# Attention heads on one core: value products in pairs of key steps instead of one step at a time

## The chip, the core and the metric

The kernel runs on one core of a Trainium2 chip. The metric is the time of one execution on the device in microseconds (us). Inputs and outputs are in DRAM, the arithmetic must be that of the reference in float32 accuracy, and everything is one program of six phases.

## What is computed

Six blocks one after another on `x` of 4 x 1024 tokens with 256 features, each adding to `x`: half a mixture of 16 experts, attention with biases, half the mixture again, half a lookup-table network, attention without biases, and half the lookup-table network again. The change touches the two attention blocks:

```python
q = (jnp.einsum('btc,oc->bto', x, Wq) + bq).reshape(Bb, Tt, H, D).transpose(0, 2, 1, 3)
...
logits = jnp.einsum('bhqd,bhkd->bhqk', q, k) / jnp.sqrt(jnp.float32(D))
causal = jnp.triu(jnp.ones((Tt, Tt), dtype=bool), 1)
logits = jnp.where(causal, -jnp.inf, logits)
attn = jax.nn.softmax(logits, axis=-1)
out = jnp.einsum('bhqk,bhkd->bhqd', attn, v)
```

There are 16 heads of 16 features, 4 batches and 1024 positions.

## The kernel before

`attention_phase` has a projection phase and then `heads_phase`, which is run twice in the program (tiles `attn_heads_...`). It works by quads: four heads of one batch, 16 quads (`NQ`) one after another. A quad holds two kinds of score products, both in bfloat16 parts stacked to a depth of 96 or 99.

- **Row scores** (`unit`, line 1101): 32 units per quad, one for each head and block of 128 queries, in the order `QUERY_ORDER = (5, 4, 1, 2, 7, 6, 0, 3)` for each head. Unit of block i has (i + 1) x 128 columns, 128 to 1024, so one product or two (at most 512 columns each), and fills one or two of the four banks of `s_ps`. VectorE (line 1299) reduces each to its row maxima. The units run a whole quad ahead: while quad n has its turned scores, the units of quad n+1 (and the first 9, `LEAD`, of n+2) are issued. In a line of the 32 units that are issued during a quad, number d (from 0) is unit 9 + d, counted around: d = 4 has 896 columns, then 128, 512, 768, 640, 256, 384, 1024 and again 896, 128, and so on. `unit` waits on `s_free` until VectorE has left the banks; `score_banks` gives each unit its banks in a ring, so that a unit of two banks waits for the last unit that had them.
- The maxima of a quad are split on GpSimd (`split_max`), turned by one product (`turn_max`, line 1111, once per quad), copied by VectorE and stored by a DMA into the stacked operands.
- **Turned scores** (`scores_t`, line 1120): 12 key steps (`STEPS`), 4 for the first half of the queries and 8 for the second, times 4 heads are 48 pieces. Widths of the steps: 512, 384, 256, 128, then five times 512, then 384, 256, 128. They go through three banks of `st_ps` (`NB`): piece p waits until ScalarE has taken the exponential of piece p - 3 (line 1218). The results go to `probs`, a ring of four steps (`NR`): the exponentials of step G wait until the value products of step G - 4 are done. On the diagonal steps (0 to 3 and 8 to 11) GpSimd then masks (line 1043).
- **Value products** (`times_v`, line 1136): per step one group, four products (one for each head), which the chip executes as eight float32 passes. The four heads stand in the four 32-column strips of TensorE and stream side by side. A group waits for the step's exponentials or mask. Each half of a quad gathers in the one bank `o_ps`, which ScalarE copies out (`copy_out`, line 1200), at the pieces in `COPY_AFTER`.

The order on TensorE is written out by three tables. After piece p (0 to 47) come the units until `PACE[p]` of them are issued, and then the value groups that `VALUES_AFTER` names for p, relative to the quad's step 0:

```python
PACE = (0, 0, 1, 2, 4, 4, 4, 5, 5, 7, 7, 7, 8, 9, 10, 11, 11, 11, 12, 13, 14, 15, 15, 16, 16, 17, 17, 18, 20, 20, 21,
        21, 23, 24, 24, 25, 25, 26, 27, 28, 28, 28, 28, 28, 29, 29, 31, 32)
```

In the last quad of a phase no units are left, and the output projection (`project`, line 1157) stands in their place. The operands of a quad (`stack0`, `more_st`) are loaded by SP two quads ahead, from the time when the turned scores of quad n begin, and the units of quad n+2 need them from piece 32 of quad n on.

Of the kernel before, what the change touches and what calls it, by code (L numbers as in the profile page):

```python
# [687 lines left out]
def step_queries(half, j):  # L688

    first = max(half * TILE, j * P)  # L690
    return first, (half + 1) * TILE - first
# [3 lines left out]

PACE = (0, 0, 1, 2, 4, 4, 4, 5, 5, 7, 7, 7, 8, 9, 10, 11, 11, 11, 12, 13, 14, 15, 15, 16, 16, 17, 17, 18, 20, 20, 21,
        21, 23, 24, 24, 25, 25, 26, 27, 28, 28, 28, 28, 28, 29, 29, 31, 32)
COPY_AFTER = (9, 28)
VALUES_AFTER = {2: -3, 5: -2, 8: -1, 12: 0, 18: 1, 22: 2, 25: 3, 31: 4, 35: 5, 38: 6, 41: 7, 44: 8}


def score_banks(quads, banks):
# [54 lines left out]
def heads_phase(nc, name, before, q_dram, k_dram, v_sb, stack0, first_loaded, o_dram, inv_dram, x_in, x_out, w_o, b_o, consts):  # L757
# [5 lines left out]
    NQ = BATCH * QUADS  # L763
    UNITS = QUAD * QT
    PIECES = QUAD * len(STEPS)
    S = len(STEPS)
# [26 lines left out]
    def masks_until(G):  # L793
        n, s = divmod(G, S)
        return n * len(DIAGONAL) + sum(d <= s for d in DIAGONAL)

    with ExitStack() as ctx:
# [130 lines left out]
        with nc.Block() as block:  # L928
# [161 lines left out]
            def _(pe):  # L1090
                def unit(g):
                    n, k = divmod(g, UNITS)
                    h, i = k // QT, QUERY_ORDER[k % QT]
                    r, (at, _, over) = n % R, UNIT_AT[g]
                    if k == 0:
                        pe.wait_ge(stack_loaded[r], LOAD * (n // R + 1))
                    if over:
                        pe.wait_ge(s_free, over)
                    for a in range(0, (i + 1) * P, TILE):
                        w = min(TILE, (i + 1) * P - a)  # L1100
                        last = pe.matmul(s_ps[:, at + a // TILE, 0:w], q_st(r)[0:DEPTH, h, i * P:(i + 1) * P],  # L1101
                                         k_st(r)[0:DEPTH, h, a:a + w], start=True, stop=True)
                    last.then_inc(s_full, 1)
                    if k == TURN_AFTER and n > 0:
                        turn_max(n - 1)

                def turn_max(m):
                    at, _, over = TURN_AT[m]
                    pe.wait_ge(parts_ready, m + 1)
                    pe.wait_ge(s_free, over)  # L1110
                    pe.matmul(s_ps[0:SPLIT * UNITS, at, 0:P], max_parts[:, m % 2, :], identb[:, :],
                              start=True, stop=True).then_inc(s_full, 1)

                def scores_t(n, s, h):
                    half, j = STEPS[s]
                    first, w = step_queries(half, j)
                    v = n * PIECES + s * QUAD + h
                    if v >= NB:
                        pe.wait_ge(exp_done, v - NB + 1)
                    pe.matmul(st_ps[:, v % NB, 0:w], k_st(n % R)[0:ROWS, h, j * P:(j + 1) * P],  # L1120
                              q_st(n % R)[0:ROWS, h, first:first + w], start=True, stop=True).then_inc(st_full, 1)

                def times_v(G):
                    n, s = divmod(G, S)
                    half, j = STEPS[s]
                    first, w = step_queries(half, j)
                    use = 2 * n + half
                    if j == 0 and use >= OB:
                        pe.wait_ge(o_free, use - OB + 1)
                    if s in DIAGONAL:  # L1130
                        pe.wait_ge(masked, masks_until(G))
                    else:
                        pe.wait_ge(exp_done, QUAD * (G + 1))
                    for h in range(QUAD):
                        at = ((n * QUAD + h) * QT + j) * VW
                        last = pe.matmul(o_ps[h * VW:(h + 1) * VW, use % OB, TILE - w:TILE], v_sb[:, at:at + VW],  # L1136
                                         probs[:, G % NR, h, 0:w], start=(j == 0), stop=(s in (SUB - 1, S - 1)))
                    last.then_inc(pv_done, 1)

                def project(q):  # L1140

                    t, s = divmod(q, SUB)
                    u = q // 2
                    if q == 0:
                        pe.wait_ge(w_ready, 1)
                        pe.wait_ge(s_free, turn_over(NQ - 1))
                    pe.wait_ge(lo_ready, KD * t + (1 if t == TILES - 1 else KD))
                    if u >= SB and q % 2 == 0:
                        pe.wait_ge(y_free, u - SB + 1)
                    toks = slice(s * P, (s + 1) * P)  # L1150
                    for kd in range(KD):
                        if t == TILES - 1 and kd == 1:
                            pe.wait_ge(lo_ready, KD * TILES)
                        pairs = [(rows_hi[:, t % 2, kd, toks], w_hi[:, kd, :]), (rows_hi[:, t % 2, kd, toks], w_lo[:, kd, :]),
                                 (rows_lo[:, t % 2, kd, toks], w_hi[:, kd, :])]
                        for n, (a, b) in enumerate(pairs):
                            last = pe.matmul(s_ps[:, u % SB, s % 2 * D:(s % 2 + 1) * D], a, b, start=(kd == 0 and n == 0),
                                             stop=(kd == KD - 1 and n == len(pairs) - 1))
                    if q % 2 == 1:
                        last.then_inc(y_full, 1)  # L1160
# [4 lines left out]
                for n in range(NQ):  # L1165
                    pe.wait_ge(neg_loaded[n % 2], 16 * (n // 2 + 1))
                    due = 0
                    for s in range(S):
                        for h in range(QUAD):
                            scores_t(n, s, h)  # L1170
                            p = s * QUAD + h
                            while due < PACE[p]:
                                g = (n + 1) * UNITS + LEAD + due
                                if g < NQ * UNITS:
                                    unit(g)
                                elif g == NQ * UNITS + TURN_AFTER:
                                    turn_max(NQ - 1)
                                due += 1
                            if p in VALUES_AFTER and n * S + VALUES_AFTER[p] >= 0:
                                times_v(n * S + VALUES_AFTER[p])  # L1180
                            if n == NQ - 1 and p in PROJECT_AFTER:
                                project(PROJECT_AFTER[p])
                for G in range((NQ - 1) * S + max(VALUES_AFTER.values()) + 1, NQ * S):
                    times_v(G)
                for q in range(len(PROJECT_AFTER), SUB * TILES):
                    project(q)
# [7 lines left out]
            def _(act):  # L1194
                def copy_out(n, half):
                    act.wait_ge(pv_done, n * S + (SUB if half == 0 else S))
                    if n > 0:

                        act.wait_ge(o_stored[half], 16 * n)
                    act.activation(oT[:, half, :], o_ps[:, (2 * n + half) % OB, :], ACT.Copy).then_inc(o_free, 1)  # L1200
# [8 lines left out]
                for n in range(NQ):  # L1209
                    for s, (half, j) in enumerate(STEPS):  # L1210
# [4 lines left out]
                        for h in range(QUAD):  # L1215
# [3 lines left out]
                                .then_inc(exp_done, 1)  # L1219
                            if s * QUAD + h == COPY_AFTER[0] and n > 0:  # L1220
                                copy_out(n - 1, 1)
                            if s * QUAD + h == COPY_AFTER[1]:
                                copy_out(n, 0)
# [1485 lines left out]
```

## Time and profile before

| | us |
|---|---|
| median of 3 runs | 2773.62 (2769.53 to 2778.78) |
| span of the profiled execution | 2889.1 |
| TensorE busy | 2486.6 (86%) |
| VectorE busy | 1963.1 (68%) |
| ScalarE busy | 1445.2 (50%) |
| GpSimd busy | 1097.0 (38%) |

The profiled execution's own time is the span of 2889.1 us, from its first to its last instruction; what lies around it is not shown. It is 115 us longer than the median of the runs without the profiler. The two heads phases lie at about 780 to 1240 us and 2165 to 2640 us of the span. Matmuls are pipelined, so their durations overlap; the distance between two starts tells what one costs.

### The profile page before, as it was taken

The numbers are of one execution on the slowest core, as the hardware profiler recorded it, in microseconds if no ns is written. First come the engines' busy times: TensorE is split into PE (matmuls) and PEld (weight loads), VectorE is DVE, ScalarE is ACT, GpSimd is POOL, SyncE is SP. The second block draws the span as 40 slices with busy tenths as digits, with TensorE's granted clock in tenths as the row PEclk, the third lists the DMA queues.
The fourth block names the chain that finished last, engine by engine and source line by source line (L and its number), as shares of the span: only waits on it lengthen the run. The fifth ranks groups of instructions, "written<-read, shape, count | busy, mean of one in ns | idle before, by whom it ended". The sixth has DMA issues, their size and how long they took to land. (4 is left out here: it accounts for less than half of the span.)

```text
span 2889.1 us, 49366 instructions
## 1 busy us (share of the span) xinstructions
PE 2486.6 (86%) x15174; PEld 1604.9 (56%) x15190; DVE 1963.1 (68%) x5524; ACT 1445.2 (50%) x3366; POOL 1097.0 (38%) x1556
## 2 busy tenths in 40 slices
PE   7885997788799999968868994899679999996998
PEld 5664996455333333446648993677553333334776
DVE  6654887665688888656646884665568887875444
ACT  3332554232287877723324552333546887874443
POOL 5663444776322222335653446662132222220000
PEclk9997998898799999978989996999788999998999
DMA  3435555555534464343345554331473354434000
GB/s 119 150 123 145 179 179 174 157 165 171 130 85 92 95 128 93 85 159 124 126 131 170 178 178 148 98 107 48 143 178 68 78 116 99 99 96 154 30 32 27
DMA packets 251508, 350.78 MB, mean 121 GB/s; under 512 B 42437, under 2 KB 200694, under 8 KB 245110
## 3 DMA queue, kind: packets, MB, share of 16 engines
q1 hardware_dynamic: 212854, 242.71, 32.2%
q0 software_dynamic: 38400, 104.91, 10.3%
q8 instruction: 132, 2.16, 0.3%
q14 instruction: 122, 1.00, 0.1%
HBM read 196.80 MB, written 149.92 MB: 120 GB/s over the span
## 5 line engine op out<-in xcount | busy, mean ns | idle before, releaser
L1299 DVE CUSTOM_DVE_ANT_0 attn_heads_masked_s<-attn_heads_s_ps,attn_heads_causal 128x768 bf16<-128x768 f32 (+7 forms) x1024 | 726.7, 754 | 143.6 <-PE attn_heads_s_ps L1101 126.6
L1218 ACT ACTIVATE attn_heads_probs<-attn_heads_st_ps 128x512 f32<-128x512 f32 (+3 forms) x1536 | 663.4, 495 | 234.1 <-PE attn_heads_st_ps L1120 220.2
L1609 POOL DMA_INDIRECT xs_dram<-moe_route_xn,rows_at x256 | 262.0, 1023 | 182.3 <-DVE rows_at L1877 110.4
L1136 PE MATMUL attn_heads_o_ps<-attn_heads_probs,attn_v_sb 128*32 128x512 f32 (+3 forms) x3072 | 329.1, 501 | 2.1 <-POOL attn_heads_probs L1043 1.9
L1043 POOL TENSOR_SCALAR_AFFINE_SELECT attn_heads_probs<-attn_heads_probs 128x512 f32<-128x512 f32 x256 | 163.0, 637 | 364.5 <-ACT attn_heads_probs L1218 359.3
L1120 PE MATMUL attn_heads_st_ps<-attn_heads_more_st 99*128 99x512 bf16 x960 | 261.7, 330 | 0.1
L1101 PE MATMUL attn_heads_s_ps<-attn_heads_more_st 96*128 96x512 bf16 (+1 forms) x960 | 246.7, 335 | 9.8 <-DMA attn_heads_more_st<-k_dram 4.8
L2105 POOL DMA_DIRECT2D ys_dram<-moe_expert_y_sb x288 | 157.3, 546 | 244.7 <-DVE moe_expert_y_sb L2223 244.2
L1120 PEld LDWEIGHTS attn_heads_st_ps<-attn_heads_more_st 99*128 99x128 bf16 x960 | 84.5, 97 | 212.7 <-ACT attn_heads_probs L1218 159.7
L2137 PE MATMUL moe_expert_gu_ps<-moe_w_hi,moe_expert_xT_hi 128*128 x576 | 189.4, 329 | 0.9 <-DVE moe_expert_xT_lo L2205 0.7
L1101 PE MATMUL attn_heads_s_ps<-attn_stack 96*128 96x512 bf16 (+2 forms) x576 | 157.6, 358 | 27.6 <-DVE attn_heads_row_max L1299 11.3
L2179 ACT ACTIVATE moe_expert_xT_hi<-moe_expert_xT_ps 128x256 fp32r<-128x256 f32 x288 | 110.7, 384 | 132.7 <-PE moe_expert_xT_ps L2123 132.2
L97 POOL DMA_INDIRECT attn_stack<-ys_dram,rows_at x128 | 147.5, 1152 | 62.9 <-issue 36.1
L2137 PE MATMUL moe_expert_gu_ps<-moe_w_hi,moe_expert_xT_lo 128*128 x576 | 164.1, 285 | 0.0
L2137 PE MATMUL moe_expert_gu_ps<-moe_w_lo,moe_expert_xT_hi 128*128 x576 | 164.0, 285 | 0.0
L97 POOL DMA_INDIRECT lut_y_sb<-ys_dram,rows_at x128 | 132.7, 1036 | 76.3 <-issue 36.1
L1120 PE MATMUL attn_heads_st_ps<-attn_stack 99*128 99x512 bf16 (+3 forms) x576 | 159.7, 335 | 0.9 <-ACT attn_heads_probs L1218 0.7
L2564 DVE SCALAR_TENSOR_TENSOR lut_hid<-lut_gate,lut_u_ps 128x512 f32<-128x512 f32 x80 | 54.9, 687 | 151.8 <-PE lut_u_ps L2397 111.8
L2205 DVE TENSOR_TENSOR moe_expert_xT_lo<-moe_expert_xT_ps,moe_expert_xT_hi 128x256 fp32r<-128x256 f32 x288 | 122.2, 424 | 50.4 <-ACT moe_expert_xT_hi L2179 47.0
L2486 ACT ACTIVATE lut_gate<-lut_g_ps 128x512 f32<-128x512 f32 x96 | 57.2, 595 | 188.2 <-PE lut_g_ps L2397 167.0
L411 PE MATMUL attn_proj_w_ps<-attn_proj_mask,attn_proj_diag 128*128 128x512 bf16 x416 | 110.2, 420 | 47.2 <-DVE attn_proj_mask L595 43.3
L2123 PE MATMUL moe_expert_xT_ps<-ident,moe_expert_x_sb 128*128 128x128 f32 x576 | 113.4, 279 | 38.2 <-DMA moe_expert_x_sb<-xs_dram 34.8
(276 smaller groups left out, 6137.0 us busy)
## 6 DMA issues: line engine op xcount, KB each, us to landing
moe_expert_x_sb<-xs_dram SPq DMA_DIRECT2D x288, 128.0 KB, 2.1
ys_dram<-moe_expert_y_sb POOLq DMA_DIRECT2D x288, 128.0 KB, 2.1
o_dram<-attn_heads_oT SPq DMA_DIRECT2D x64, 256.0 KB, 5.7
moe_route_w_raw<-in_L_ffn_we_dram SPq DMA_DIRECT2D x96, 128.0 KB
q_dram<-attn_proj_parts SPq DMA_DIRECT2D x32, 384.0 KB, 2.8
k_dram<-attn_proj_parts SPq DMA_DIRECT2D x32, 384.0 KB, 2.7
x_mid<-moe_route_x_sb SPq DMA_DIRECT2D x16, 512.0 KB
attn_v_sb<-o_dram SPq DMA_DIRECT2D x32, 256.0 KB
```

The lines of the kernel that those rows point to most:

```text
L97: pool.indirect_dma_start(y_sb[:, r, k, :], None, ys_dram, bass.IndirectOffsetOnAxis(rows_at[:, u, k:k + 1], 0))\
L1043: pool.affine_select(out=d, in_=d, compare_op=ALU.is_ge, fill=0.0, base=0, pattern=[[0, QUAD], [1, P]], channel_multiplier=-1).then_inc(ma ...
L1101: last = pe.matmul(s_ps[:, at + a // TILE, 0:w], q_st(r)[0:DEPTH, h, i * P:(i + 1) * P], k_st(r)[0:DEPTH, h, a:a + w], start=True, stop=True)
L1120: pe.matmul(st_ps[:, v % NB, 0:w], k_st(n % R)[0:ROWS, h, j * P:(j + 1) * P], q_st(n % R)[0:ROWS, h, first:first + w], start=True, stop=Tr ...
L1136: last = pe.matmul(o_ps[h * VW:(h + 1) * VW, use % OB, TILE - w:TILE], v_sb[:, at:at + VW], probs[:, G % NR, h, 0:w], start=(j == 0), stop ...
L1218: act.activation(probs[:, G % NR, h, 0:w], st_ps[:, v % NB, 0:w], ACT.Exp, scale=scale)\
L1299: dve.tensor_tensor_reduce(out=masked_s[:, use % 4, 0:w], in0=s_banks[:, at * TILE:at * TILE + w], in1=causal[:, SEQ - w:SEQ], scale=1.0, ...
L1609: pool.indirect_dma_start(xs_dram, bass.IndirectOffsetOnAxis(rows_at[:, n * SUB + s, k:k + 1], 0), xn[:, n % RX, s, :], None).then_inc(sca ...
L2105: pool.dma_start(ys_dram[s * P:(s + 1) * P, :], y_sb[:, s % AHEAD, :]).then_inc(y_stored[s % AHEAD], 16)
L2123: last = pe.transpose(xT_ps[:, s % 2, kd * P:(kd + 1) * P], x_sb[:, s % AHEAD, kd * P:(kd + 1) * P], ident[:, :])
L2137: last = pe.matmul(gu_ps[:, s % 2, 0:D], a, b, start=(n == 0), stop=(n == len(pairs) - 1))
L2205: dve.tensor_tensor(xT_lo[:, s % RH, :, :].rearrange("p k t -> p (k t)"), xT_ps[:, s % 2, 0:D], xT_hi[:, s % RH, :, :].rearrange("p k t -> ...
```

## The change

Two tables and the loops that read them. Value groups stand after six pieces of a quad, two at each, instead of one after each of twelve pieces; the copy of the first half moves from piece 28 to piece 25. The instructions on ScalarE, VectorE, GpSimd and SP are the same in the same order, except for that copy's place. `PACE` and the number of instructions stay as they are.

```diff
-COPY_AFTER = (9, 28)
-VALUES_AFTER = {2: -3, 5: -2, 8: -1, 12: 0, 18: 1, 22: 2, 25: 3, 31: 4, 35: 5, 38: 6, 41: 7, 44: 8}
+COPY_AFTER = (9, 25)
+VALUES_AFTER = {6: (-2, -1), 14: (0, 1), 22: (2, 3), 30: (4, 5), 38: (6, 7), 46: (8, 9)}
...
-                            if p in VALUES_AFTER and n * S + VALUES_AFTER[p] >= 0:
-                                times_v(n * S + VALUES_AFTER[p])
+                            for step in VALUES_AFTER.get(p, ()):
+                                if n * S + step >= 0:
+                                    times_v(n * S + step)
...
-                for G in range((NQ - 1) * S + max(VALUES_AFTER.values()) + 1, NQ * S):
+                for G in range((NQ - 1) * S + max(VALUES_AFTER[max(VALUES_AFTER)]) + 1, NQ * S):
                     times_v(G)
```

TensorE, pieces 10 to 14 of a quad (`s_ps` row scores, `st_ps` turned scores, `o_ps` value products; the widths behind the names; x4 is one group of four heads). Before:

```order
L1101 MATMUL attn_heads_s_ps<-attn_heads_more_st 128x512
L1120 MATMUL attn_heads_st_ps<-attn_stack 128x256 x2
L1120 MATMUL attn_heads_st_ps<-attn_stack 128x128
L1101 MATMUL attn_heads_s_ps<-attn_heads_more_st 128x512
L1101 MATMUL attn_heads_s_ps<-attn_heads_more_st 128x256
L1136 MATMUL attn_heads_o_ps<-attn_heads_probs,attn_v_sb 32x512 x4
L1120 MATMUL attn_heads_st_ps<-attn_stack 128x128
L1101 MATMUL attn_heads_s_ps<-attn_heads_more_st 128x512
L1101 MATMUL attn_heads_s_ps<-attn_heads_more_st 128x128
L1120 MATMUL attn_heads_st_ps<-attn_stack 128x128
L1101 MATMUL attn_heads_s_ps<-attn_heads_more_st 128x256
```

And with the change:

```order
L1101 MATMUL attn_heads_s_ps<-attn_heads_more_st 128x512
L1120 MATMUL attn_heads_st_ps<-attn_stack 128x256 x2
L1120 MATMUL attn_heads_st_ps<-attn_stack 128x128
L1101 MATMUL attn_heads_s_ps<-attn_heads_more_st 128x512
L1101 MATMUL attn_heads_s_ps<-attn_heads_more_st 128x256
L1120 MATMUL attn_heads_st_ps<-attn_stack 128x128
L1101 MATMUL attn_heads_s_ps<-attn_heads_more_st 128x512
L1101 MATMUL attn_heads_s_ps<-attn_heads_more_st 128x128
L1120 MATMUL attn_heads_st_ps<-attn_stack 128x128
L1101 MATMUL attn_heads_s_ps<-attn_heads_more_st 128x256
L1136 MATMUL attn_heads_o_ps<-attn_heads_probs,attn_v_sb 32x512 x4
L1136 MATMUL attn_heads_o_ps<-attn_heads_probs,attn_v_sb 32x384 x4
```

The group of step 0 moved from behind piece 12 to behind piece 14, and that of step 1 joined it there; the row scores of 640 and 256 columns now stand ahead of both.

TensorE again, pieces 38 to 41, with the groups of steps 6 and 7. Before:

```order
L1120 MATMUL attn_heads_st_ps<-attn_heads_more_st 128x384
L1101 MATMUL attn_heads_s_ps<-attn_heads_more_st 128x384
L1136 MATMUL attn_heads_o_ps<-attn_heads_probs,attn_v_sb 32x512 x4
L1120 MATMUL attn_heads_st_ps<-attn_heads_more_st 128x384
L1101 MATMUL attn_heads_s_ps<-attn_heads_more_st 128x512 x2
L1120 MATMUL attn_heads_st_ps<-attn_heads_more_st 128x256 x2
L1136 MATMUL attn_heads_o_ps<-attn_heads_probs,attn_v_sb 32x512 x4
L1120 MATMUL attn_heads_st_ps<-attn_heads_more_st 128x256 x2
```

And with the change:

```order
L1120 MATMUL attn_heads_st_ps<-attn_heads_more_st 128x384
L1101 MATMUL attn_heads_s_ps<-attn_heads_more_st 128x384
L1136 MATMUL attn_heads_o_ps<-attn_heads_probs,attn_v_sb 32x512 x8
L1120 MATMUL attn_heads_st_ps<-attn_heads_more_st 128x384
L1101 MATMUL attn_heads_s_ps<-attn_heads_more_st 128x512 x2
L1120 MATMUL attn_heads_st_ps<-attn_heads_more_st 128x256 x4
L1120 MATMUL attn_heads_st_ps<-attn_heads_more_st 128x128
```

The group of step 7 moved from behind piece 41 to behind piece 38, and between that run and the next one stand pieces 39 to 46 alone with their units.

## Rows read from the trace of the kernel before

**Rows 1.** The page, part 1: busy us (share of the span) and instructions.

```profile
PE 2486.6 (86%) x15174; PEld 1604.9 (56%) x15190; DVE 1963.1 (68%) x5524; ACT 1445.2 (50%) x3366; POOL 1097.0 (38%) x1556
```

**Rows 2.** Timeline of TensorE, maxima products: start us, us, engine, line, operation.

```profile
1002.23 0.22 PE L1111 MATMUL attn_heads_s_ps<-identb,attn_heads_max_parts 128*96 128x128 bf16 x1
...
1028.92 0.22 PE L1111 MATMUL attn_heads_s_ps<-identb,attn_heads_max_parts 128*96 128x128 bf16 x1
```

**Rows 3.** One quad: length; PE, PEld, DVE, ACT, POOL busy; PEclk, DMA share, GB/s.

```profile
1002.23:1028.92 26.69, 26.69 (x195) 9.53 (x194) 22.95 (x65) 21.43 (x51) 5.98 (x12) 1.00 0.41 81
```

**Rows 4.** Waits in that quad: waiter, releaser, us in total, times, longest.

```profile
ACT attn_heads_probs L1218 <- PE attn_heads_st_ps L1120: 5.5, 11, 1.0
DVE attn_heads_masked_s L1299 <- PE attn_heads_s_ps L1101: 3.7, 10, 1.0
...
PEld attn_heads_s_ps L1101 <- DVE attn_heads_row_max L1299: 0.9, 4, 0.3
```

**Rows 5.** Timeline of TensorE, pieces 12 to 22 of a quad.

```profile
1014.42 1.06 PE L1136 MATMUL attn_heads_o_ps<-attn_heads_probs,attn_v_sb 128*32 128x512 f32 x8
1015.42 0.23 PE L1120 MATMUL attn_heads_st_ps<-attn_heads_more_st 99*128 99x128 bf16 x1
...
1017.39 0.85 PE L1136 MATMUL attn_heads_o_ps<-attn_heads_probs,attn_v_sb 128*32 128x384 f32 x8
...
1019.27 0.38 PE L1101 MATMUL attn_heads_s_ps<-attn_stack 96*128 96x512 bf16 x1
1019.49 0.38 PE L1120 MATMUL attn_heads_st_ps<-attn_heads_more_st 99*128 99x512 bf16 x1
1019.80 0.64 PE L1136 MATMUL attn_heads_o_ps<-attn_heads_probs,attn_v_sb 128*32 128x256 f32 x8
1020.37 0.39 PE L1120 MATMUL attn_heads_st_ps<-attn_heads_more_st 99*128 99x512 bf16 x1
```

**Rows 6.** Timeline of TensorE and its weight loads, end of the first phase.

```profile
1232.44 1.79 PE L1136 MATMUL attn_heads_o_ps<-attn_heads_probs,attn_v_sb 128*32 128x384 f32 x24
1232.79 0.13 PEld L1136 LDWEIGHTS attn_heads_o_ps<-attn_heads_probs,attn_v_sb 128*32 128x32 f32 x4 [0.19 <-issue]
1233.11 0.13 PEld L1136 LDWEIGHTS attn_heads_o_ps<-attn_heads_probs,attn_v_sb 128*32 128x32 f32 x4 [0.19 <-issue]
```

**Rows 7.** Timeline of VectorE; in brackets its idle time before.

```profile
1012.81 1.09 DVE L1299 CUSTOM_DVE_ANT_0 attn_heads_masked_s<-attn_heads_s_ps,attn_heads_causal 128x896 bf16<-128x896 f32 x1 [0.25 <-PE attn_heads_s_ps L1101]
...
1013.83 0.29 DVE L1299 CUSTOM_DVE_ANT_0 attn_heads_masked_s<-attn_heads_s_ps,attn_heads_causal 128x128 bf16<-128x128 f32 x1
...
1014.04 0.69 DVE L1299 CUSTOM_DVE_ANT_0 attn_heads_masked_s<-attn_heads_s_ps,attn_heads_causal 128x512 bf16<-128x512 f32 x1
...
1015.96 0.82 DVE L1299 CUSTOM_DVE_ANT_0 attn_heads_masked_s<-attn_heads_s_ps,attn_heads_causal 128x640 bf16<-128x640 f32 x1 [0.35 <-PE attn_heads_s_ps L1101]
...
1016.71 0.42 DVE L1299 CUSTOM_DVE_ANT_0 attn_heads_masked_s<-attn_heads_s_ps,attn_heads_causal 128x256 bf16<-128x256 f32 x1
...
1017.05 0.55 DVE L1299 CUSTOM_DVE_ANT_0 attn_heads_masked_s<-attn_heads_s_ps,attn_heads_causal 128x384 bf16<-128x384 f32 x1
...
1017.53 1.22 DVE L1299 CUSTOM_DVE_ANT_0 attn_heads_masked_s<-attn_heads_s_ps,attn_heads_causal 128x1024 bf16<-128x1024 f32 x1
```

**Rows 8.** Timeline of ScalarE, exponentials, merged by threes.

```profile
1008.64 1.57 ACT L1218 ACTIVATE attn_heads_probs<-attn_heads_st_ps 128x512 f32<-128x512 f32 x3 [0.33 <-PE attn_heads_st_ps L1120]
...
1014.25 0.84 ACT L1218 ACTIVATE attn_heads_probs<-attn_heads_st_ps 128x256 f32<-128x256 f32 x3
```

**Rows 9.** Timelines of TensorE and VectorE where a bank is waited for.

```profile
935.77 0.28 PE L1101 MATMUL attn_heads_s_ps<-attn_stack 96*128 96x256 bf16 x1
...
935.64 0.82 DVE L1299 CUSTOM_DVE_ANT_0 attn_heads_masked_s<-attn_heads_s_ps,attn_heads_causal 128x640 bf16<-128x640 f32 x1
```

**Rows 10.** Second phase: TensorE behind a stack's arrival, and its clock after.

```profile
2442.87 0.82 PE L1101 MATMUL attn_heads_s_ps<-attn_heads_more_st 96*128 96x512 bf16 x2 [3.80 <-DMA attn_heads_more_st<-k_dram]
...
2443.00:2446.00 3.00, 3.00 (x14) 0.81 (x12) 1.80 (x4) 1.08 (x2) 0.64 (x1) 0.50 0.02 7
```

## The prediction

> **What bounds the kernel now.** I read the page first: TensorE is busy 86% of the span, VectorE 68%, ScalarE 50% [rows 1]. That is an average over six phases, so I went on to the only stretches that the edit touches, the two heads phases of 16 quads each (about 800 to 1235 and 2180 to 2626 us). The turned maxima, one product per quad, mark the period: 26.69 us from one to the next [rows 2]. In such a quad TensorE has no gap (26.69 us busy of 26.69) and the granted clock is 1.00, VectorE is busy 22.95 and ScalarE 21.43 [rows 3]. The waits of the same quad say how near the other two are: VectorE stands idle 3.7 us for want of scores, ScalarE 5.5 us, and TensorE's score products wait 0.9 us for banks [rows 4]. So TensorE bounds the quad, with VectorE 14% behind and ScalarE 20%, and these two are fed out of rings that hold little: four banks of row scores for VectorE (two units, roughly), three of turned scores for ScalarE.
>
> **What is removed.** In the timeline of TensorE [rows 5] 512-wide score products start 0.22 us apart, but the value product behind one starts 0.31 us after it: 0.09 us to change over. Four heads' value products of 512 columns take 1.00 us to the next product's start, those of 256 columns 0.57: 0.43 per 256 columns and 0.14 beside. One changeover and back is 0.09 + 0.14 = 0.23 us, and the rows are rounded, so 0.24. Do two groups one behind the other save it? The end of the phase shows it [rows 6]: there three groups already stand together. The second group's weight loads, one pass ahead of its products, start at 1232.79 and 1233.11, 0.32 us apart, which is one 384-column pass and nothing more ((0.43 x 1.5) / 2). So the whole 0.24 us goes. Per phase there are 190 changeovers (16 x 12, less two joined at the end), and 96 after. 2 x 94 x 0.24 = 45 us of TensorE's own time, 1.44 us per quad, to 25.25. The Trainium skill, TensorEngine Tiling (Array Packing), Key Properties, says that changing the tiling mode drains the engine; by that rule alone the change gives these 45 us, and the trace agrees that the drain is there. That is my first rival, not my forecast.
>
> **What is added: gaps in the supply.** No instruction is added, and no DMA is moved. But the two feeds now stop for both groups together: steps 0,1 for 0.09 + 0.85 + 0.64 + 0.14 = 1.73 us; 2,3 for 0.88; 4,5 and 6,7 for 1.95; 8,9 for 1.73; 10,11 for 0.88. Before, the longest stop was 1.00 + 0.09 = 1.09 us. VectorE needs, unit following unit, 1.02 us for 896 columns, 0.75 for 640, 0.48 for 384, 0.34 for 256, 0.21 for 128 [rows 7], and by the same slope 0.61 for 512, 0.88 for 768 and 1.15 for 1024. ScalarE needs 0.49 us per 512 columns (three in 1.57, the last one alone 0.60) and about 0.28 per 256 [rows 8]; by interpolation 0.39 for 384 and 0.17 for 128, and 0.5 for a copy. TensorE streams 0.22 us per 512 columns [rows 5], others in proportion.
>
> I walked one quad of the new order by these numbers, always in order: a product starts when its engine is free and its bank is (0.12 us after VectorE, 0.15 after ScalarE), the reader starts 0.2 us after the product's stream. The latencies are read so: piece 13 starts at 1015.42, its 0.06 us and the 0.27 of the 640-column unit behind it end at 1015.75, and VectorE begins that unit at 1015.96 [rows 5, 7], 0.2 later; VectorE left the 768-column unit at 935.64 and the product that needed its bank began at 935.77, 0.13 later [rows 9]. ScalarE's 0.15 is my estimate by the latter. The worst stretch, pieces 7 to 14, counted from the end of the run of steps 10,11: VectorE still works until 0.22; TensorE streams piece 7 and the 896-column unit until 0.55, so VectorE idles to 0.75 and has it until 1.77; the 128 and 512 units follow until 2.58. The 768 unit needs the banks of the 896 one, so it starts at 1.89 though TensorE was ready at 1.65; VectorE has it from 2.58 to 3.46. The 640 unit waits for the 512 one (2.70), the 256 one for the 768 one: it starts at 3.58, TensorE having been ready at 3.03. Only then, at 3.78, can the run of steps 0,1 start, and it ends at 5.42. TensorE's own work there is 0.79 (turned scores) + 1.36 (six units) + 1.73 = 3.88 us. 1.5 us are lost, and while the run lasts VectorE has 0.75 + 0.34 us left to do and then nothing: it idles near 1.3 us.
>
> The other stretches by the same walk, TensorE's own time and the walk's: pieces 15 to 22, 3.71 and 4.37; 23 to 30, 5.37 and 6.14 (here ScalarE, with the copy after piece 25 in its way, holds back pieces 29 and 30); 31 to 38, 4.73 and 5.32 (ScalarE, idle at the start since its three banks last 1.5 us of a 1.95 us run); 39 to 46, 3.60 and 4.26; 47 to 6, 3.60 and 4.02. Sum: 24.9 own, **29.53 us per quad**, against 26.69: +2.84. The loss comes from how little is buffered, not from the engines' rates. As a test I walked pieces 13 to 22 of the old order likewise: it gives 2.40 us between the runs of steps 1 and 2, and in the trace they lie 2.41 apart (1017.39 and 1019.80 of rows 5).
>
> **The sum.** Units are issued alongside in 14.6 quads of each phase: 2 x 14.6 x 2.84 = +83 us. The last quad of a phase has no units and saves up to 6 x 0.24 = 1.4 us, twice: -3. The stack of a later quad arrives late in some quads: in the second phase TensorE stood 3.80 us for it, and behind that the clock granted to it was 0.50, half of the 2.4 GHz [rows 10]; two such quads there, two smaller ones in the first phase. A slower quad reaches the stack's first unit some 2.5 us later, so the waits shrink: about -1 in the first phase, -5 in the second, and perhaps -3 for products no longer streamed at the lower clock. Together +71 us. Against the profiled execution's span of 2889.1 us that is 2960; the unprofiled median is 2773.6, 115 us less, and since the heads phases run at full clock there I take their change over unscaled: **2844 us**, +2.6%. Other costs I put at nothing: the ring of four probability tiles (a step's slot is freed by a run ahead of the piece that needs it, at each of the six places), GpSimd's masks (0.64 us each, done over 1 us before the run that reads them), the move of the copy from piece 28 to 25 (inside the walk). If the masks lost that cover, it would be tenths of a us per quad.
>
> Bounds: nothing here shows a run of two long groups beside VectorE's feed, so the lower end is that half of the walk's waits are overstated (+1.4 per quad: +41, less 7, so +34, 2808), and the upper that each latency is 0.1 us longer at some ten blocked starts (+3.8 per quad: +111, less 7, so +104, 2878).
>
> **Rivals.** (a) The feeds have slack enough and TensorE stays the bound: VectorE 23.0 of 25.25 us. For it: the averages of rows 3 and the small wait of 0.9 us in rows 4. Against: with two units' worth of banks (1.1 us in front of steps 0,1) a stop of 1.73 us can't be bridged; the point at which it decides is whether the 256-column unit ahead of that run waits for the 768 one. 2773.6 - 45 = 2729 us, faster. Chance 7%. (b) Gain and gaps cancel: VectorE and ScalarE catch up within a quad and the waits are a third of the walk's, 1.5 us; 2773 within 8 us. 4%. (c) As my forecast, and the waits also lower the clock: had each quad 3 us at 0.50 as behind the stack's wait of rows 10, that is 1.5 us each, +44: about 2888 us. Against: no wait in the walk is longer than 0.7 us. 8%. (d) The groups don't join, because the second one's semaphore wait parts them: then 45 us more than the forecast; rows 6 speak against, 2%.
>
> **The numbers.** The forecast has 79%. The range from 2808 to 2878 takes in its bounds and stops short of (c). A measurement of this kernel can tell about 0.3% (8 us) from no change. Faster by more: 7%; within: 4%; slower by more: 89%.
>
> **What would show it.** The products of the maxima lie 29 to 30 us apart, not 25.3 (a) or 26.7 (b). TensorE's waits for VectorE in a quad rise from 0.9 us to over 2, VectorE's idle time from 3.7 to above 6, ScalarE's to 8. Value products stand in runs of 16 without a gap, 1.95 us long for steps 4,5. The granted clock stays at 1.00 in both phases; phases outside of the heads keep their times. The forecast is wrong if the period is under 28 us, or if it grows while VectorE's idle time does not.

## The result, and the profile after

| | before | changed |
|---|---|---|
| median (lowest to highest) of 4 runs, us | 2773.3 (2769.53 to 2778.78) | 2872.31 (2868.65 to 2885.24) |
| span of the profiled execution, us | 2889.1 | 2872.1 |
| one quad (plain, in either phase), us | 26.69 | 29.92 and 30.21 in turn |

The change makes the kernel slower: the ratio is 1.0351, with a 95% interval of 1.0319 to 1.0383, or +99 us. The forecast was 2844 us, in the range 2808 to 2878.

The two profiled spans can't be set against each other: in the profiled execution of before everything outside of the two heads phases took longer, 2004 us against 1895. The first of the turned maxima comes at 788.2 us there and at 728.1 in the profile of the change, with nothing edited ahead of it. Later I took a second trace of before (e9), which has it at 727.9; all differences of spans below are against that one.

The page of the changed kernel, part 1, and from part 5 the row of VectorE's reductions:

```profile
PE 2494.1 (87%) x15174; PEld 1613.6 (56%) x15190; DVE 1961.4 (68%) x5524; ACT 1429.6 (50%) x3366; POOL 1100.1 (38%) x1556
...
L1300 DVE CUSTOM_DVE_ANT_0 attn_heads_masked_s<-attn_heads_s_ps,attn_heads_causal 128x768 bf16<-128x768 f32 (+7 forms) x1024 | 723.2, 754 | 237.0 <-PE attn_heads_s_ps L1101 221.8
```

The busy times are those of before to about 1% [rows 1]: nothing was added. The idle time of the readers tells of the change: 237.0 us in front of the 1024 reductions, of which 221.8 is ended by a row score, where the page of before (there line 1299) has 143.6 and 126.6; and 340.9 us in front of ScalarE's exponentials, where it was 234.1.

The timeline of TensorE, the turned maxima of two quads in the first phase, and the window between the next two of them (its length; busy PE, PEld, DVE, ACT, POOL; clock, DMA share, GB/s):

```profile
999.06 0.26 PE L1111 MATMUL attn_heads_s_ps<-identb,attn_heads_max_parts 128*96 128x128 bf16 x1
...
1029.99 0.26 PE L1111 MATMUL attn_heads_s_ps<-identb,attn_heads_max_parts 128*96 128x128 bf16 x1
...
1059.91 0.26 PE L1111 MATMUL attn_heads_s_ps<-identb,attn_heads_max_parts 128*96 128x128 bf16 x1
...
1029.99:1059.91 29.92, 28.35 (x195) 10.27 (x193) 22.79 (x66) 20.87 (x52) 10.77 (x15) 1.00 0.49 110
```

From the second to the third it is 29.92 us where it was 26.69 [rows 2]. VectorE and ScalarE do the same work as in the quad before, 22.79 and 20.87 us [rows 3], TensorE is no longer without a gap (28.35 of 29.92), and the clock is 1.00 as it was. (The quad from 999.06 to 1029.99, 30.93 us, has four more instructions of VectorE in it, 70 in place of 66. It holds no wait for a stack: the trace of the change shows none in either heads phase.)

The waits of that quad (waiter, releaser; us in total, times, longest):

```profile
ACT attn_heads_probs L1219 <- PE attn_heads_st_ps L1120: 8.8, 9, 2.2
...
DVE attn_heads_masked_s L1300 <- PE attn_heads_s_ps L1101: 7.1, 8, 2.0
PEld attn_heads_st_ps L1120 <- ACT attn_heads_probs L1219: 6.2, 21, 0.5
...
PEld attn_heads_s_ps L1101 <- DVE attn_heads_row_max L1300: 2.5, 7, 0.9
PE attn_heads_s_ps L1101 <- DVE attn_heads_row_max L1300: 0.8, 2, 0.5
...
PEld attn_heads_s_ps L1111 <- POOL attn_heads_max_parts L1037: 0.2, 1, 0.2
```

Against rows 4, ScalarE's wait goes from 5.5 to 8.8 us, VectorE's from 3.7 to 7.1, and that of TensorE's weight loads for VectorE from 0.9 to 2.5. They wait for each other in turn: no engine is full, which fits rings that are too short for the runs; the experiments test it. The weight loads of the turned scores wait for ScalarE too, 6.2 us here. That isn't new: in the quad of before it is 8.0 us, a wait that rows 4 leave out, and it passes there while TensorE still streams other products:

```profile
PEld attn_heads_st_ps L1120 <- ACT attn_heads_probs L1218: 8.0, 15, 0.8
```

The stretch that the prediction called the worst, pieces 7 to 14, in the timeline of TensorE (start, us, operation, columns, and in brackets the idle time before it):

```profile
1043.69 0.45 PE L1101 MATMUL attn_heads_s_ps<-attn_heads_more_st 96*128 96x512 bf16 x2
1043.97 0.22 PE L1120 MATMUL attn_heads_st_ps<-attn_heads_more_st 99*128 99x128 bf16 x1
1044.57 0.28 PE L1101 MATMUL attn_heads_s_ps<-attn_heads_more_st 96*128 96x256 bf16 x1 [0.38 <-DVE attn_heads_row_max L1300]
1044.78 1.71 PE L1136 MATMUL attn_heads_o_ps<-attn_heads_probs,attn_v_sb 128*32 128x512 f32 x16
1046.42 0.23 PE L1120 MATMUL attn_heads_st_ps<-attn_heads_more_st 99*128 99x128 bf16 x1
```

and in that of VectorE:

```profile
1043.55 0.95 DVE L1300 CUSTOM_DVE_ANT_0 attn_heads_masked_s<-attn_heads_s_ps,attn_heads_causal 128x768 bf16<-128x768 f32 x1
...
1044.42 0.82 DVE L1300 CUSTOM_DVE_ANT_0 attn_heads_masked_s<-attn_heads_s_ps,attn_heads_causal 128x640 bf16<-128x640 f32 x1
...
1045.17 0.42 DVE L1300 CUSTOM_DVE_ANT_0 attn_heads_masked_s<-attn_heads_s_ps,attn_heads_causal 128x256 bf16<-128x256 f32 x1
...
1046.86 0.56 DVE L1300 CUSTOM_DVE_ANT_0 attn_heads_masked_s<-attn_heads_s_ps,attn_heads_causal 128x384 bf16<-128x384 f32 x1 [1.26 <-PE attn_heads_s_ps L1101]
```

VectorE is done with the 768-column unit when its next one starts, at 1044.42; 0.15 us later the 256-column unit, which needs its banks, is streamed, and right behind it the run of steps 0,1: sixteen passes without a gap from 1044.78 to 1046.42. While it lasts VectorE works off what it has and then stands idle 1.26 us. Both were in the prediction (the wait, and an idle time near 1.3 us).

### The profile page after: what moved, and what is told of

The parts are those of the page before. It is cut to its first block and busy times, and to the rows that moved or that the text cites. A ratio compares the mean times of both kernels' runs of the same rounds, so it can differ in the third digit from the quotient of the medians.

```text
span 2872.1 us, 49366 instructions
## 1 busy us (share of the span) xinstructions
PE 2494.1 (87%) x15174; PEld 1613.6 (56%) x15190; DVE 1961.4 (68%) x5524; ACT 1429.6 (50%) x3366; POOL 1100.1 (38%) x1556
## 5 line engine op out<-in xcount | busy, mean ns | idle before, releaser
L1300 DVE CUSTOM_DVE_ANT_0 attn_heads_masked_s<-attn_heads_s_ps,attn_heads_causal 128x768 bf16<-128x768 f32 (+7 forms) x1024 | 723.2, 754 | 237.0 <-PE attn_heads_s_ps L1101 221.8
L1219 ACT ACTIVATE attn_heads_probs<-attn_heads_st_ps 128x512 f32<-128x512 f32 (+3 forms) x1536 | 646.3, 504 | 340.9 <-PE attn_heads_st_ps L1120 333.8
L1120 PE MATMUL attn_heads_st_ps<-attn_heads_more_st 99*128 99x512 bf16 x960 | 283.5, 332 | 12.8 <-ACT attn_heads_probs L1219 7.6
L1136 PE MATMUL attn_heads_o_ps<-attn_heads_probs,attn_v_sb 128*32 128x512 f32 (+3 forms) x3072 | 293.4, 499 | 1.1 <-POOL attn_heads_probs L1043 1.0
L1101 PE MATMUL attn_heads_s_ps<-attn_heads_more_st 96*128 96x512 bf16 (+1 forms) x960 | 254.3, 337 | 28.1 <-DVE attn_heads_row_max L1300 25.4
L1120 PEld LDWEIGHTS attn_heads_st_ps<-attn_heads_more_st 99*128 99x128 bf16 x960 | 90.6, 97 | 223.0 <-ACT attn_heads_probs L1219 124.2
L1120 PE MATMUL attn_heads_st_ps<-attn_stack 99*128 99x512 bf16 (+3 forms) x576 | 170.5, 338 | 7.0 <-ACT attn_heads_probs L1219 4.7
L1136 PEld LDWEIGHTS attn_heads_o_ps<-attn_heads_probs,attn_v_sb 128*32 128x32 f32 x3072 | 80.4, 109 | 139.5 <-issue 90.4
```

Source lines behind the costliest of these rows:

```text
L1219: act.activation(probs[:, G % NR, h, 0:w], st_ps[:, v % NB, 0:w], ACT.Exp, scale=scale)\
L1300: dve.tensor_tensor_reduce(out=masked_s[:, use % 4, 0:w], in0=s_banks[:, at * TILE:at * TILE + w], in1=causal[:, SEQ - w:SEQ], scale=1.0, ...
```

## Where the 99 us lie

Against the second trace of before, the span is 91.6 us longer. From the first exponential of a heads phase to its last it is 486.8 and 489.9 us, against 444.8 and 442.5: +89.5, so nearly all. Quad by quad (from each quad's first exponential to the next quad's), with what the prediction had counted for the same quads:

| quads of both phases | measured | predicted |
|---|---|---|
| 22 plain ones (1 to 8, 10 to 12) | +78.1 | 22 x 2.84 = +62.5 |
| the first of each phase | +8.5 | +5.7 |
| 9 and 13, in which before waited for a stack | -3.1 | 4 x 2.84 - 9 = +2.4 |
| 14 | +7.4 | 2 x 0.6 x 2.84 = +3.4 |
| the last | -1.5 | -3 |
| sum | +89.5 | +71 |

Four of these quads are 1.6 us longer than their like: 13 of the first phase, and 1, 5 and 13 of the second. In each of them the clock granted to TensorE falls to 0.50, its lower level of 1.2 GHz, for 3.4 us. That is 3.3 of the 78.1 us of the plain quads, and 3.3 in the row of 9 and 13. Quad 5 of both phases and the stretch inside the second:

```profile
886.46:916.79 30.33, 28.35 (x195) 10.26 (x194) 23.68 (x70) 20.87 (x50) 6.01 (x13) 1.00 0.49 103
2274.00:2305.97 31.97, 29.92 (x195) 10.69 (x194) 23.68 (x70) 20.93 (x51) 6.01 (x13) 0.95 0.45 97
2282.20:2285.40 3.20, 3.20 (x17) 0.90 (x10) 0.86 (x6) 0.60 (x2) 0.64 (x1) 0.50 0.80 136
```

Each fall comes with the wait of the 256-column unit for its bank or right behind it, at the run of steps 0,1. In quad 1 of the second phase that run takes 3.15 us in place of 1.71:

```profile
2158.91 0.28 PE L1101 MATMUL attn_heads_s_ps<-attn_heads_more_st 96*128 96x256 bf16 x1 [0.38 <-DVE attn_heads_row_max L1300]
2159.12 3.15 PE L1136 MATMUL attn_heads_o_ps<-attn_heads_probs,attn_v_sb 128*32 128x512 f32 x16
```

The same wait stands in every quad that issues units (0.38 us, and 0.79 in quads 5, 9 and 13, where VectorE has four more instructions), and the clock falls in four of them only. So the wait isn't all of the cause; no run tests it. In e9 the clock falls three times for as long, each time behind a wait for a stack.

## Experiments

Two theories stood at the start. **Supply**: the runs of two groups are longer than what the rings hold, so the waits between the engines make the loss, and it goes when a feed gets quicker, a run shorter, or the units around a run are placed for it. **TensorE itself**: value products joined in this way cost it more, whatever the feeds do (a changeover that isn't saved, a lower rate). Each run gives the period of a quad, which is reproducible to 0.01 us between traces and chips, and so tells more than the time of the whole.

**e1_vector_half.** The changed kernel; VectorE reduces only the first half of the columns of each unit (and masks none), so the maxima are not those of the rows.

```diff
+                    w //= 2
-    dve.tensor_tensor_reduce(out=masked_s[:, use % 4, 0:w], ..., in1=causal[:, SEQ - w:SEQ],
+    dve.tensor_tensor_reduce(out=masked_s[:, use % 4, 0:w], ..., in1=causal[:, 0:w],
```

> The changed order, with VectorE reducing only the first half of each row-score unit (without the causal mask). The walk of one quad, done with VectorE's time as 0.075 us plus half of its slope, gives 28.1 us per quad against 29.7 by the same walk (30.1 in the trace). Theory 'gaps in the feeds': 28.2 to 28.7 us per quad, ScalarE's waits left. Rival 'the lost time is TensorE's own': no change, 30.1.

Measured: 2813.21 us in one run (before beside it 2777.32). Window of one quad:

```profile
897.57:926.11 28.54, 27.74 (x196) 10.00 (x194) 14.52 (x65) 20.76 (x52) 8.41 (x14) 1.00 0.55 115
```

VectorE is busy 14.52 us in place of 22.79 and the quad falls from 30.07 (mean of the two lengths) to 28.54. VectorE's rate was under the loss, though it had over 7 us idle in every quad; but only for 1.53 of the 3.38 us.

**e2_scalar_half.** The same with ScalarE: exponentials of the first half of the columns of each piece alone, the rest of `probs` filled with 1.0 once.

```diff
-    act.activation(probs[:, G % NR, h, 0:w], st_ps[:, v % NB, 0:w], ACT.Exp, scale=scale)
+    act.activation(probs[:, G % NR, h, 0:w // 2], st_ps[:, v % NB, 0:w // 2], ACT.Exp, scale=scale)
```

> The changed order, with ScalarE taking the exponential of only the first half of each piece's columns (the rest of the probabilities keep ones). The walk gives 29.2 us per quad against 29.7; theory: 29.3 to 29.8, since VectorE's banks hold TensorE back in most stretches. If ScalarE were the one that is short, it would be below 28.5. Rival 'TensorE's own': 30.1.

Measured: quads of 29.24 and 29.74 us, 0.6 less than the change; the time was 2876.96 us (the fill is in it). ScalarE alone gives little.

**e3_both_quarter** and **e4_single_both_quarter.** Both edits, at a quarter of the columns, in the changed order and in the order of before. What remains is TensorE's own work in both orders.

> The changed order, VectorE and ScalarE reading a quarter of the columns each: both feeds are then far ahead. The walk gives 25.5 us per quad, which is TensorE's own time (24.9 of streams and changeovers, and a few short waits). If the joined groups saved nothing, it would be 26.9.

> The order before, VectorE and ScalarE reading a quarter of the columns each. The walk gives 26.5 us per quad against 26.69 in the trace of before. The difference to the same cut of the changed order is what joining is worth by itself: 1.0 us by the walk, at most 6 x 0.24 = 1.44; nothing if the groups don't join.

Measured: 2745.21 and 2768.16 us. A quad each, e3 first:

```profile
860.38:886.09 25.71, 25.50 (x195) 10.60 (x195) 10.70 (x71) 11.05 (x51) 5.94 (x13) 1.00 0.61 128
```
```profile
859.99:886.41 26.42, 26.42 (x196) 9.73 (x195) 10.80 (x69) 11.29 (x51) 5.93 (x12) 1.00 0.60 124
```

With quick feeds the joined order is the faster one, 25.71 against 26.42 us. So joined products cost TensorE nothing more: the theory that they do falls, and the changed kernel's 4.4 us above that (30.07 to 25.71) go when VectorE and ScalarE are quick: they are the waits for these two. But joining is worth only 0.71 us per quad here, half of the 1.44 of the prediction and less than the 1.0 of the walk. The Trainium skill (TensorEngine Tiling (Array Packing), Key Properties) says that a change of the tiling mode drains the engine. These two runs agree so far that six changes fewer each way gain something, about 0.7 us a quad, which the real feeds don't let through.

**e5_long_pairs** and **e6_short_pairs.** `PACE` as it is and the copy behind piece 28 as before, some groups joined and all others single: in e5 the two long pairs (4,5 and 6,7), in e6 the two shortest (2,3 and 10,11).

```diff
-VALUES_AFTER = {6: (-2, -1), 14: (0, 1), 22: (2, 3), 30: (4, 5), 38: (6, 7), 46: (8, 9)}
+VALUES_AFTER = {2: (-3,), 5: (-2,), 8: (-1,), 12: (0,), 18: (1,), 22: (2,), 25: (3,), 30: (4, 5), 38: (6, 7), 44: (8,)}
...
+VALUES_AFTER = {2: (-3,), 5: (-2, -1), 12: (0,), 18: (1,), 22: (2, 3), 31: (4,), 35: (5,), 38: (6,), 41: (7,), 44: (8,)}
```

> The order before, with only the groups of steps 4,5 and 6,7 joined (behind pieces 30 and 38), all else as before. TensorE's own time falls by 2 x 0.24 = 0.48 us per quad, so the rival 'TensorE stays the bound' says 26.2. The walk says 28.0 us per quad (it is 0.3 short in the changed kernel, so 27.9 to 28.4): the two longest runs alone carry 1.2 to 1.6 us of the 3.4.

> The order before, with only the short groups joined: steps 2,3 behind piece 22 and steps 10,11 behind piece 5 (runs of 0.64 us of streams). 'TensorE stays the bound': 26.2 us per quad. The walk: 26.9, no change within 0.2 against 26.69, because the units that stood between them now come too early for their banks: the table of the units would have to be moved with them.

Measured: 2908.03 and 2890.82 us, on a chip where before took 2882.83 us (that chip takes 100 us more outside of the heads). Quads of 27.79 and 28.14 us in e5, +1.28 on before; of 26.97 in e6, +0.28. The turned maxima of e6:

```profile
914.92 0.22 PE L1111 MATMUL attn_heads_s_ps<-identb,attn_heads_max_parts 128*96 128x128 bf16 x1
942.16 0.22 PE L1111 MATMUL attn_heads_s_ps<-identb,attn_heads_max_parts 128*96 128x128 bf16 x1
969.12 0.22 PE L1111 MATMUL attn_heads_s_ps<-identb,attn_heads_max_parts 128*96 128x128 bf16 x1
```

The cost grows with the length of the runs: two of about 1.9 us cost 1.28 us a quad (the walk had 28.0, and the mean is 27.97), two of about 0.9 us 0.28. Even a short pair costs more than it saves where the units around it stay as they were.

**e10_copy28.** The change with `COPY_AFTER = (9, 28)`, as before.

> The changed order with the copy of the first half back behind piece 28. The walk: 29.6 us per quad against 29.7, so 30.0 against 30.1 in the trace: the moved copy is no cause, whatever the theory. If the copy behind piece 25 were what holds ScalarE back (pieces 29 and 30), it would be 29.4 or less.

Measured: 2863.66 us, quads of 29.71 and 30.00. The moved copy costs 0.2 us per quad and isn't the cause.

**e7_pairs_paced.** All six pairs as in the change, but `PACE` and the copy placed for them, by the prediction's walk.

```diff
-PACE = (0, 0, 1, 2, 4, 4, 4, 5, 5, 7, 7, 7, 8, 9, 10, 11, 11, 11, 12, 13, 14, 15, 15, 16, 16, 17, 17, 18, 20, 20, 21,
-        21, 23, 24, 24, 25, 25, 26, 27, 28, 28, 28, 28, 28, 29, 29, 31, 32)
+PACE = (1, 3, 3, 4, 4, 5, 5, 6, 8, 8, 8, 8, 9, 10, 10, 10, 11, 12, 13, 13, 13, 15, 15, 16, 17, 17, 17, 18, 20, 20, 21,
+        23, 24, 24, 25, 25, 26, 27, 28, 29, 29, 29, 29, 30, 31, 32, 32, 32)
-COPY_AFTER = (9, 25)
+COPY_AFTER = (8, 27)
```

> The changed order's six joined runs, with the table of the units (and the places of the two copies) fitted to them by the walk. If the loss were only a table that no longer fits, it would go away (25.3 us per quad). The walk says 27.7, with its error 27.7 to 28.1 us per quad: about two thirds of the loss go, and it stays above the order before, since six stops of up to 1.95 us outlast the banks at any table.

Measured: 2916.3 us (the chip of e5), quads of 28.13 and 27.93 us. Moving the units and the copies alone takes back 2.04 of the 3.38 us (the copy's move of e10 was worth 0.2). What is left, +1.34 us on before, no placement that I found by the walk removes: it was the best of those walked, not of all.

**e8_mix.** Only pairs 2,3 (behind 23) and 10,11 (behind 7 of the next quad) joined, with `PACE` and the copy placed for them.

```diff
+PACE = (0, 1, 3, 4, 4, 5, 5, 5, 7, 7, 8, 8, 9, 10, 11, 12, 12, 12, 13, 13, 16, 16, 16, 17, 17, 20, 20, 20, 21, 23, 23,
+        24, 24, 25, 26, 26, 26, 26, 28, 28, 28, 28, 29, 31, 31, 31, 32, 32)
+VALUES_AFTER = {1: (-3,), 7: (-2, -1), 12: (0,), 19: (1,), 23: (2, 3), 28: (4,), 32: (5,), 36: (6,), 40: (7,), 45: (8,)}
```

> Only the short groups joined (steps 2,3 behind piece 23 and steps 10,11 behind piece 7 of the next quad), the eight others single, and the table of the units and the copies fitted by the walk. TensorE's own time is 25.97 - 0.48 us and the longest stop stays at 1.09 us. The walk: 26.2 us per quad against 26.8 for the order before, so 26.1 to 26.4, and 30 x 0.45 = 13 us off the kernel: 2756 to 2766 us against 2773, if the stacks' waits don't grow by the same. Rival 'every joining costs': above 26.7.

Measured: 2885.88 us (median of 11 runs; a twelfth took 2904.51) against 2882.83 (17 runs of before on that chip), ratio 0.9998, interval 0.9968 to 1.0028: no difference, where I had expected 13 us. The quads are shorter than those of before, 26.45 us against 26.69, but over 26 quads that is only 6 us, and part of it is lost elsewhere: quad 14 takes 25.75 us in place of 25.11, and TensorE still stands idle for the stacks. In quad 9:

```profile
1036.31 0.50 PE L1100 MATMUL attn_heads_s_ps<-attn_heads_more_st 96*128 96x512 bf16 x2 [2.31 <-DMA attn_heads_more_st<-k_dram]
```

Quads 9 and 13 last 31.00, 33.21, 30.89 and 32.99 us, as they wait for their stack to arrive: together 22.3 us over four plain ones, where before has 18.8 in its first trace and 21.2 in e9. A quicker quad comes sooner to a DMA that is late. Both heads phases together take 883.3 us, against 884.7 and 887.3 in the two traces of before; a gain of this size the times of whole runs can't tell.

**e9_before_again.** The kernel before, unchanged, for its trace on a chip like that of the change.

> The kernel before once more, for a trace beside the others of the same chip. 26.69 us per quad; heads phases of 439 to 446 us. On a chip where the kernel before takes 2775 us all of the 99 us of the change should lie in the two heads phases: 487 and 490 us in the changed kernel, so 440 to 445 each here, and the other phases as long as in the changed kernel within 10 us.

Measured: 2782.19 us; quads of 26.69, and quads 9 and 13 of 32.79, 32.46, 33.01 and 29.67: 21.2 us more than four plain ones. TensorE's products stand idle for stacks for 14.1 us of these:

```profile
PE attn_heads_s_ps L1101 <- DMA attn_heads_more_st<-k_dram: 7.8, 2, 4.3
...
PE attn_heads_s_ps L1101 <- DMA attn_stack<-k_dram: 6.3, 2, 3.7
```

The wait in quad 9 of the first phase, in the timeline of TensorE:

```profile
997.60 0.76 PE L1101 MATMUL attn_heads_s_ps<-attn_heads_more_st 96*128 96x512 bf16 x2 [3.44 <-DMA attn_heads_more_st<-k_dram]
```

**e11_mix_loads** and **e12_single_loads.** In front of that late stack, SP's queue has the loads of `x` for two token tiles (`load_x`, in `output_ahead`), issued in quads 8 and 12. Both kernels issue them behind the next quad's stack load; e11 in the order of e8, e12 in that of before. (`add_bias`, which works on the loaded `x`, moves a quad later.)

```diff
-BIAS_IN = (1, 2, 3, 9, 10, 13, 14)
+BIAS_IN = (1, 2, 3, 10, 11, 14, 15)
...
-                            if b > 1:
-                                load_x(RX + t - HALVES)
-                                load_x(RX + t - HALVES + 1)
...
                         load(n + 2)
+                        if n > QUADS + 1 and n % QUADS == 1:
+                            t = (n // QUADS - 1) * HALVES
+                            load_x(RX + t - HALVES)
+                            load_x(RX + t - HALVES + 1)
```

> The mixed order of e8 (26.45 us per quad), and SP issues the residual rows' loads of later batches behind the stack's loads of the next quad in place of ahead of them (and the biases are added one quad later). In e8 quads 9 and 13 took 31.0, 33.2, 30.9 and 33.0 us: 22 us more than the others, waiting for a stack. Theory: the stack lands 4 to 6 us earlier, so 10 to 16 of the 22 us go and the mix's 0.24 us per quad shows: 0.6 to 0.8% faster than before. Rival: the rows of the last batch, which stay ahead, are what delays the stack: nothing gained over e8, within 0.3% of before.

> The order before (single groups, 26.69 us per quad) with the residual rows' loads behind the stack's, as in e11. It parts e11's gain: if the stack's waits are most of it (they were 21 of 25 us in the two heads phases of the kernel before, quads 9 and 13), this is 0.4 to 0.8% faster than before on its chip, and quads 9 and 13 take under 28 us; the mixed order's own share is then 0.24 us x 26 = 6 us, 0.2%. Rival: the mixed order carries e11's gain, and this stays within 0.2% of before.

Measured: e11 2760.3 us (2758.03 to 2767.7, 6 runs), ratio to before 0.995, interval 0.993 to 0.9969; e12 2764.71 (2756.03 to 2768.05, 6 runs), ratio 0.9949, interval 0.993 to 0.9969. Both are faster than the kernel before by 0.5% (e11 was expected at 0.6 to 0.8%), and than the changed one. Quads 9 and 13 last 26.98, 27.08, 26.89 and 26.89 us in e11 and 26.93 to 27.05 in e12: no product waits for a stack any more in either. In the traces both heads phases together are 21 us shorter in e12 than in e9; the medians on its chip differ by 13 us, and what makes the rest I don't know. A quad of e11:

```profile
938.55:965.00 26.45, 26.45 (x196) 10.15 (x195) 22.82 (x66) 21.34 (x51) 6.00 (x12) 1.00 0.41 82
```

The joined short pairs of e11 make a plain quad 0.24 us shorter besides (heads phases of 431.2 and 431.6 us against 432.9 and 433.2 in e12), which the times of whole runs can't tell: 4.4 us between the medians, within their spread and on two chips.

## Why the prediction was right, and by how much it was off

- **What bounds the kernel: right.** TensorE without a gap at 26.69 us before; e4, with both other engines busy for only 11 us of a quad, is at 26.42, so the feeds cost the old order 0.27.
- **What is removed, 0.24 us for each changeover, 1.44 per quad: too high in effect.** The groups do join without a gap (x16 above), as rows 6 had said. But with quick feeds the order gains 0.71 us (e3, e4), or 0.92 if TensorE's busy time is taken (25.50 against 26.42), so 0.12 to 0.15 for each changeover. Part of the "0.14 beside" read off the rows of before may be work that overlaps otherwise in the joined order; no run measured a changeover alone, so this stays open.
- **The walk: right in mechanism, 12 to 19% short in the loss.** It gave 29.53 us; 29.92 and 30.21 came. By stretch, measured against walked: pieces 7 to 14 5.46 and 5.42, 15 to 22 4.41 and 4.37, 23 to 30 6.20 and 6.14, 31 to 38 5.47 and 5.32, 39 to 46 4.32 and 4.26, 47 to 6 4.06 and 4.02. The rest of each second quad, 0.29 us, I didn't follow, since I walked one quad and the lengths come in turns of two. The term "29.53, +2.84 per quad" is thus what was mis-sized: +3.38. TensorE's own time in the walk was short as well: its stretches sum to 24.9 us, the prediction's other road gave 25.25, and e3 shows 25.50 busy. How much of the miss comes from that isn't shown. The largest miss of a stretch has the turned maxima in it, and there stands a wait that I hadn't walked. The line of that product in the changed kernel (what ended its idle time: us, times):

```profile
L1111 PE MATMUL attn_heads_s_ps<-identb,attn_heads_max_parts x32: 257/257/314, 728.1 to 2571.1; 128*96 128x128 bf16 x32
its engine sat idle before it (us, times) until:
  POOL attn_heads_max_parts L1037: 7.3, 32
```

Before, the same product stood idle 0.3 us in all. VectorE now gives up the last maxima of a quad later against the product, and GpSimd's four steps (1058.71 to 1059.87 in the quad above) end just behind it: 0.23 us in each of 32 quads. It is absent in e6 and all but absent in e1. That it makes up the miss isn't shown: no run took it away alone, it is nearly all a wait of the product's weight load (PEld), in front of which the timeline of the products has no gap, and in e5 it is there (6.7 us in 29 quads) though the walk isn't short.
- **+83 us for 2 x 14.6 quads:** the first of each phase costs 4.2 to 4.4 us and quad 14 3.7, where I had counted 0.6 of 2.84. Quads 1 and 5 of the second phase were 1.6 us longer than their like in the first, by the fall of the clock to 0.50 (above), which the sum didn't have.
- **Stack waits -1, -5, and -3 for the clock: the waits right in sign and too small, the clock wrong.** What quads 9 and 13 take over plain ones shrinks by 16.6 us against e9 (from 21.2 to 4.6), where I had 9. The waits for stacks are wholly gone: a slower quad forgives the late DMA. The clock gave nothing back: three stretches of 3.4 us at 0.50 in e9, four in the changed kernel, and two of these four make up most of the 4.6.
- **The last quads, -3:** -1.5. There, too, joining gave half of the counted price.
- **Rivals.** (a) TensorE stays the bound, 2729 us, by the rule of the drain alone: refuted, and e3 shows the condition under which it would have held. (b) Cancelling: refuted here; e8 is the case in which gain and new waits nearly do. (c) The clock falls: it did, in four of 32 quads for 1.6 us each, so 6.6 us and not 44. The argument against it, no wait above 0.7 us, didn't hold either: the wait of 0.79 us above comes six times. Its 2888 us lie near what was measured, but mainly by another road. (d) Groups that don't join: refuted.
- **The signs:** waits of TensorE for VectorE over 2 us (2.5), VectorE's above 6 (7.1), ScalarE's about 8 (8.8), runs of 16, and phases outside of the heads that keep their times (1895 us against 1893 in e9) came. The period of 29 to 30 came in every second quad (29.92; the others 30.21 and more). The clock of 1.00 in both phases did not: see the four falls.
- **The range, and luck.** The bounds take 7 us off where the sum takes 12 (3, 6 and 3); with 12 the range would be 2803 to 2873, and 2872 at its very edge. Errors also went against each other: the walk and the first quads were short by 18 us and more, the waits for stacks shrank by 7 or 8 more than said. Had the waits shrunk only as said, the time would by my estimate have been about 2880 us (2872 and those 7 or 8), just outside. The sign and the mechanism are not luck (e3, e7); that the number fell inside the range partly is.

The errors of the walk went the same way, to longer. A walk with each latency at its read value has no rest for what it doesn't model: the quads in turns of two, the maxima's chain, the rest of TensorE's own time.

## What to carry to other kernels

An engine that is busy 100% of a stretch can still lose by a change that gives it less to do: compare the longest run in which it feeds nobody with what its readers have in their rings, not the busy times. Here runs of 1.7 to 1.95 us stood against rings of about 1 to 1.5 us, and 14 to 20% of slack in VectorE and ScalarE did not help. Join groups only where the run stays inside the ring, place the supply anew around it, and first look for a late transfer, which can be worth more: moving two loads behind the stack's gave 0.5% in the old order, and the best joining nothing that could be told.

Not tried: deeper rings. `s_ps` has four banks, `st_ps` three and `o_ps` one, and none of them was enlarged.

## What the runs showed beyond that

- The chips differ by about 100 us (2777 and 2883 for the same kernel), and outside of the heads phases: there e5 to e8, on the slower chip, spend 1992 to 2003 us, the other runs 1889 to 1916. The kernel before has a quad of 26.69 us in all three traces (before, e9, e12), though the first has 2004 us outside and e9 1893. The period within a phase carries over; a difference of two spans doesn't.
- Halving the work of an engine with 7 us of idle time in each 30 us took 1.53 us off the quad (e1): idle time doesn't prove that an engine costs nothing, where it stands idle in turns with another.
- The maxima's product before takes 0.22 us and in the changed kernel 0.26; both are the modelled ends of pipelined records, and I draw nothing from it.
